# A routed expert layer on one core: five fixed experts' weights loaded from the last scores on, and TensorE's read of a tile's expert moved ahead of the wait before it

## The chip, the core and the metric

One core of one Trainium2 chip runs the kernel. The metric is the device time of one execution in microseconds; three runs of the kernel before gave 484.14, 484.23 and 485.39 us, median 484.23.

## What is computed

Two residual layers on x of 32 x 128 x 256 floats. First a gated attention over a context of the same shape, batch by batch (32 batches of 128 tokens, 16 heads of 16). Then a mixture of 14 experts over all 4096 tokens, each token going to one:

```python
x = x + tanh(g_xattn) * attention(layernorm(x), ctx, ctx)        # 16 heads, causal
h = layernorm(x).reshape(-1, 256)
logits = h @ router_w                                            # 256 x 14
weight, expert = softmax(logits) at its argmax
hid = gelu(h @ w1[expert] + b1[expert])                          # 256 -> 512
out = hid @ w2[expert] + b2[expert]                              # 512 -> 256
x = x + tanh(g_ffn) * out * weight
```

## The kernel before

The program is written engine by engine, each with its own list of instructions, and every hand-over is a semaphore. A first part runs a pipeline over the 32 batches: projections, scores, exponentials, transposed probabilities, attention, the dense layer, the router, and the token's row and name written to DRAM, sorted by expert. GpSimd scatters the names, SyncE loads inputs and stores rows.

The second part works on 39 slots (`SLOTS`). The first 25 (`FULL`) are full slots: 128 tokens of one expert. Their rows are fetched by GpSimd with an indirect DMA (`fetch`), normalised by VectorE (`norm`), transposed by TensorE (`up_in`), copied by VectorE (`up` there), multiplied by the expert's first weights (`up` of TensorE, 16 products), put through gelu by ScalarE, multiplied by the second weights (`down`, 8 products), and added up by VectorE (`start_out`, `result`), and stored by GpSimd (`store`). Slots 0 to 9 (`EARLY`) are made of the first 24 batches, so they can begin while the last batches are in attention. First weights come into a ring of R = 5 buffers (`w_ring`, 642 KB each, `load_up`); second weights of all 14 experts lie in `W2` from early on.

The last 14 slots are half slots: 64 tokens of an expert that is looked up and 64 of a fixed one, slot 25 + j taking expert j. The fixed expert's first weights, 512 KB each, are the "residents": `load_resident(e)` on SyncE puts expert e into `W1[:, e, :]`. `W1` has no memory of its own. It lies over the arena that holds the attention's buffers, expert e on columns 1024 e to 1024 e + 1023 of the arena, so a resident may be loaded only when whatever `part(n)` put on these columns is no longer used. `hold(base_ready, n)` lets SyncE wait until VectorE has begun the output of slot n - 1.

What sets the order around the change:

- SyncE's list after the last pipeline step: names of the slots 0 to 4, ring weights 0 to 4, stores 27 and 28, names of slots 5 to 9, stores 29 and 30, ring weights 5 and 6, store 31, the biases, residents 0 to 2, ring weights 7 to 9, names of slots 10 to 24, residents 3 and 4, the names of the half slots in two loads each, residents 5 to 13. It is one queue: what waits holds up all behind it.
- GpSimd's list: fetch of slot s + 5 behind the start of slot s, and the stores of results.
- TensorE's list in slots 4 to 9: `down(s)`, `up(s + 2)`, `up_in(s + 3)`. In full slots from 10 on: `up_in(s + 2)`, `up(s + 1)`, `down(s)`. In half slots: `half_up(s + 2)`, `turn(s + 1)`, `up_in(s + 3)`, `half_down(s)`.
- Every down product first reads the number of its expert from `slot_expert` or `half_expert` into a register of TensorE's sequencer (`value_load`, lines 1457 and 1506). In `down` this is ahead of its two waits, in `half_down` behind them.

Lines: 438 residents, 443 ring weights on SyncE, 424 and 432 names, 420 row stores, 595 row fetches, 604 result stores, 1078 `norm`, 1072 VectorE's `up`, 1095 `result`, 1057 the second table of slots, 1453 `up_in`, 1466 `up`, 1475 `down`, 1489 and 1491 `half_up`, 1499 `turn`, 1508 and 1511 `half_down`, 1547 the scores.

Of the kernel before, what the change touches and what calls it, by code (L numbers as in the profile page):

```python
# [7 lines left out]
P = 128  # L8
B = 32
D = 256  # L10
# [9 lines left out]
E = 14  # L20
# [114 lines left out]
def flamingo_kernel(nc, x, ctxt, gates, wq, wk, wv, wd, wd_turned, bqk, bv, bd, bd_column, rw, w1b, b1, w2, consts, out):  # L135
# [5 lines left out]
    with ExitStack() as ctx:  # L141
# [68 lines left out]
        wv_sb = part(DC * D).rearrange("p (c n) -> p c n", c=DC)  # L210
        wd_sb = part(DC * WIDE).rearrange("p (c n) -> p c n", c=DC)
# [5 lines left out]
        x_in = part(4 * D).rearrange("p (r d) -> p r d", r=4)  # L217
        c_in = part(4 * D).rearrange("p (r c s) -> p r c s", r=4, c=DC)
        x_biased = part(4 * D).rearrange("p (r d) -> p r d", r=4)
        xn = part(2 * D).rearrange("p (r d) -> p r d", r=2)  # L220
# [3 lines left out]
        k_masked = part(2 * DC * HT * P).rearrange("p (r c v s) -> p r c v s", r=2, c=DC, v=HT)  # L224
# [171 lines left out]
        def _(sp):  # L396
# [93 lines left out]
            for k in range(R):  # L490
                hold(names_loaded[k], 16)
                load_names(k, R + k)
            store(batch(29))
            store(batch(30))
            next_up(5)
            next_up(6)
# [3 lines left out]
            for e in range(3):  # L500
                load_resident(e)
# [8 lines left out]
            load_resident(3, 11)  # L510
            load_resident(4, 15)
# [4 lines left out]
            load_resident(5, 19)  # L516
            load_resident(6, 23)
            for e in range(7, E):
                load_resident(e, 26 + 3 * (e - 7) // 2)
# [911 lines left out]
        def _(pe):  # L1431
# [38 lines left out]
            def down(r, s):  # L1470
                ex = expert(s)
                pe.wait_ge(hid_t_ready, s + 1)
                wait(pe, out_ready, s - 1)
                for ch in range(FC):
                    ins = pe.matmul(y_bank[r][:, 0:D], hid_t[:, RING[r], ch, :],  # L1475
                                    W2[:, bass.ds(ex, 1), ch, :].rearrange("p e n -> p (e n)"),
                                    start=(ch == 0), stop=(ch == FC - 1))
                ins.then_inc(y_done, 1)
# [23 lines left out]
            def half_down(s):  # L1502

                pe.wait_ge(hid_t_ready, s + 1)
                pe.wait_ge(out_ready, s - 1)
                ex = pe.value_load(half_expert[0:1, s - FULL:s - FULL + 1], min_val=0, max_val=E - 1)
                for ch in range(FC):
                    pe.matmul(y_bank[s % R][0:HALF, 0:D], hid_t[:, RING[s % R], ch, 0:HALF],  # L1508
                              W2[:, bass.ds(ex, 1), ch, :].rearrange("p e n -> p (e n)"),
                              start=(ch == 0), stop=(ch == FC - 1))  # L1510
                    ins = pe.matmul(y_bank[s % R][HALF:P, 0:D], hid_t[:, RING[s % R], ch, HALF:P], W2[:, s - FULL, ch, :],
                                    start=(ch == 0), stop=(ch == FC - 1))
                ins.then_inc(y_done, 1)

            def full_slot(s):

                up_in((s + 2) % R, s + 2)
# [4 lines left out]
                down(s % R, s)  # L1522

            def mixed_slot(s):

                if s + 2 < SLOTS:
                    half_up(s + 2)
# [4 lines left out]
                if s < FULL:  # L1532
                    down(s % R, s)
                else:
                    half_down(s)
# [230 lines left out]
            down(0, 0)  # L1766
# [5 lines left out]
            down(1, 1)  # L1772
# [8 lines left out]
            down(2, 2)  # L1781
            up(4, 4)
            up_in(0, 5)
            down(3, 3)
            up(0, 5)
            lines(FULL - EARLY, 2).then_inc(slot_lines, 1)
            up_in(1, 6)

            for s in range(4, EARLY - 1):
                down(s % R, s)  # L1790
                up((s + 2) % R, s + 2)
                up_in((s + 3) % R, s + 3)
            down(4, 9)
# [57 lines left out]
```

## Time and profile before

| | us |
|---|---|
| median of three runs | 484.23 |
| the profiled execution, own time | 488.7 |
| its span, first to last instruction | 486.8 |
| TensorE matmul busy | 462.1 (95%) |
| VectorE busy | 351.3 (72%) |
| ScalarE busy | 314.2 (65%) |
| GpSimd busy | 304.5 (63%) |

The profiled execution moved 65.68 MB by DMA, 135 GB/s over its span. Its page also gives the span in 40 slices, and the slices around two thirds of the span are those in which the share of busy DMA engines rises from 0.2 to 0.8 and more, and in which TensorE's share, 0.9 or more nearly everywhere, falls to 0.8. Times in all rows are microseconds from the first instruction. PE is TensorE's matmul, PEld its weight load, PEldq its sequencer on that side, DVE VectorE, ACT ScalarE, POOL GpSimd, SPq the instructions with which SyncE issues DMAs. An entry such as `x8 [0.41 <-issue]` says eight instructions in a row, with 0.41 us of idle time before the first, ended by nothing that the profile shows.

### The profile page before, as it was taken

The page shows a single profiled execution, that of the slowest core. Times are in us where ns is not written, and L with a number is a line of the kernel's source. Part 1 is how long each engine was busy: PE and PEld are TensorE (multiplying, and loading weights), DVE is VectorE, ACT ScalarE, POOL GpSimd, SP SyncE. Part 2 cuts the span into 40 slices and gives each one's busy share as a digit, 9 for nine tenths or more (in the row PEclk, how much of TensorE's full clock was granted, in tenths as well). Part 3 has the DMA queues.
Part 4 walks back from the last instruction along what each step waited for, and adds up shares of the span by engine and source line. Part 5 has one row for each costly group of instructions (what it writes and reads, how often), then busy time and mean ns, then how long its engine had stood idle before and what let it go on. Part 6 is the DMA issues. An engine that isn't in the chain of part 4 may idle for free.

```text
span 486.8 us, 16417 instructions
## 1 busy us (share of the span) xinstructions
PE 462.1 (95%) x4775; PEld 371.3 (76%) x4775; DVE 351.3 (72%) x1128; ACT 314.2 (65%) x1481; POOL 304.5 (63%) x668
## 2 busy tenths in 40 slices
PE   8999999999999999999999998888799999999991
PEld 4888888888888888888888886776689998555540
DVE  3678999898898898998998987664345544555640
ACT  2589899889899898898898897341223322244340
POOL 5475577686776776777777676574556565445321
PEclk9899999999999999999999999998999999999997
DMA  7263566312212212212111272389778888899700
GB/s 238 78 217 134 145 179 158 54 40 47 51 37 45 52 33 52 46 32 65 34 44 36 68 213 73 92 234 290 227 222 265 259 253 247 299 300 280 243 9 7
DMA packets 38765, 65.68 MB, mean 135 GB/s; under 512 B 12457, under 2 KB 27055, under 8 KB 38704
## 3 DMA queue, kind: packets, MB, share of 16 engines
q1 hardware_dynamic: 26272, 35.33, 26.4%
q10 hardware_dynamic: 7424, 19.60, 12.6%
q0 software_dynamic: 5008, 10.01, 7.2%
q8 instruction: 29, 0.48, 0.4%
q14 instruction: 32, 0.26, 0.2%
HBM read 55.84 MB, written 9.99 MB: 135 GB/s over the span
## 4 chain that ended last, share of the span: by engine, by line
PE 80%; ACT 6%; issue 4%; DVE 4%; DMA 3%; POOL 1%; POOLq 0%; ACTq 0%; DVEq 0%
PE bank L1555 11%; PE bank L1624 10%; PE bank L1475 9%; PE bank L1466 8%; PE bank L1614 6%; ACT arena L851 5%; PE bank L1547 5%; PE bank L1508 5%; PE bank L1563 5%; PE bank L1692 5%; PE bank L1489 5%; PE bank L1610 2%; PE bank L1453 2%; PE bank L1542 2%; DMA g_rows<-token_rows,fetch_idx 2%
## 5 line engine op out<-in xcount | busy, mean ns | idle before, releaser
L851 ACT ACTIVATE arena<-bank,negmax 128x128 f32<-128x128 f32 x512 | 179.6, 403 | 13.0 <-DVE negmax L1129 13.0
L851 ACT ACTIVATION_READ_ACCUMULATOR arena<-bank,negmax 128x1 f32 x512 | 124.2, 243 | 0.0
L1129 DVE TENSOR_REDUCE negmax<-bank 128x4 f32<-128x512 f32 x128 | 84.5, 682 | 9.9 <-PE bank L1547 8.9
L1555 PE MATMUL bank<-C,arena 128*128 128x128 f32 x512 | 78.9, 277 | 1.7 <-ACT arena L851 1.2
L604 POOL DMA_INDIRECT out<-g_out,g_name x39 | 39.2, 1006 | 64.9 <-DVE g_name L1084 47.4
L809 ACT ACTIVATE hid_t<-bank,w_ring 128x128 f32<-128x128 f32 x100 | 28.5, 369 | 72.6 <-PE bank L1466 52.3
L1624 PE MATMUL bank<-arena 128*128 128x128 f32 x512 | 71.6, 283 | 0.4 <-ACT arena L877 0.2
L1555 PEld LDWEIGHTS bank<-C,arena 128*128 128x128 f32 x512 | 60.5, 141 | 12.2 <-ACT arena L851 2.4
L1624 PEld LDWEIGHTS bank<-arena 128*128 128x128 f32 x512 | 62.7, 193 | 8.0 <-issue 7.0
L1095 DVE SCALAR_TENSOR_TENSOR g_out<-bank,g_name,g_out 128x256 f32<-128x256 f32 x39 | 18.8, 483 | 59.8 <-PE bank L1475 24.6
L859 ACT ACTIVATE arena<-bank 128x512 f32<-128x512 f32 x64 | 40.8, 638 | 24.6 <-PE bank L1555 24.3
L1475 PE MATMUL bank<-W,hid_t 128*128 x200 | 49.8, 394 | 3.6 <-issue 3.5
L1466 PE MATMUL bank<-g_xt,w_ring 128*128 128x128 f32 x400 | 48.9, 275 | 1.2 <-issue 1.0
L1466 PEld LDWEIGHTS bank<-g_xt,w_ring 128*128 128x128 f32 x400 | 47.2, 192 | 2.5 <-issue 2.1
L595 POOL DMA_INDIRECT g_rows<-token_rows,fetch_idx x39 | 39.5, 1012 | 11.0 <-issue 7.1
L574 POOL DMA_INDIRECT token_names<-name,pos x32 | 34.5, 1077 | 16.6 <-issue 13.0
L1475 PEld LDWEIGHTS bank<-W,hid_t 128*128 128x128 f32 x200 | 36.9, 194 | 10.1 <-issue 5.9
L1137 DVE COPY arena<-bank 128x512 f32<-128x512 f32 x64 | 43.6, 681 | 1.4 <-PE bank L1555 0.4
L834 ACT ACTIVATE hid_t<-bank,w_ring 128x64 f32<-128x64 f32 x56 | 18.3, 327 | 37.7 <-issue 23.8
L620 POOL COPY arena<-rinv 128x128 f32<-128x128 f32 x64 | 17.1, 294 | 40.8 <-DVE rinv L1186 40.8
L583 POOL TENSOR_TENSOR arena<-arena,C 128x256 f32<-128x256 f32 x64 | 37.7, 605 | 2.5 <-ACT arena L877 2.5
L1614 PE MATMUL bank<-arena 128*128 128x270 f32 x128 | 37.1, 411 | 0.0
(179 smaller groups left out, 997.9 us busy)
## 6 DMA issues: line engine op xcount, KB each, us to landing
w_ring<-w1b ACTq DMA_DIRECT2D x15, 642.0 KB
w_ring<-w1b ACTq DMA_DIRECT2D x14, 514.0 KB
W<-w SPq DMA_DIRECT2D x14, 512.0 KB
arena<-w1b SPq DMA_DIRECT2D x14, 512.0 KB, 4.1
w_ring<-w1b SPq DMA_DIRECT2D x10, 642.0 KB
token_rows<-rows SPq DMA_DIRECT2D x32, 129.0 KB
arena<-x SPq DMA_DIRECT2D x32, 128.0 KB
arena<-ctxt SPq DMA_DIRECT2D x31, 128.0 KB, 3.8
```

Source lines behind the costliest of these rows:

```text
L583: ins = pool.tensor_tensor(k_masked[:, n.par, ch, :, :], k_t[:, ch, :].rearrange("p (o s) -> p o s", o=1).to_broadcast([P, HT, P]), const( ...
L595: pool.indirect_dma_start(out=g_rows[:, r, :], out_offset=None, in_=source, in_offset=bass.IndirectOffsetOnAxis(ap=fetch_idx[:, r:r + 1], ...
L604: pool.indirect_dma_start(out=out_rows, out_offset=bass.IndirectOffsetOnAxis(ap=g_name[:, r, 0:1], axis=0), in_=g_out[:, r, :], in_offset= ...
L851: ins = act.activation(probs[:, q, v, :], bank[q][:, v * P:(v + 1) * P], ACT.Exp, bias=negmax[:, b.par, h:h + 1], accum_out=rsum[:, b.par, ...
L859: act.activation(probs_t[:, q, :, :].rearrange("p v s -> p (v s)"), bank[4 + q % 2][:, :], ACT.Copy).then_inc(probs_t_scalar, 1)
L1129: dve.tensor_reduce(negmax[:, b.par, q * HQ:(q + 1) * HQ], bank[q][:, :].rearrange("p (v k) -> p v k", v=HQ), axis=AX_X, op=ALU.max, negat ...
L1137: dve.tensor_copy(probs_t[:, q, :, :].rearrange("p v s -> p (v s)"), bank[4 + q % 2][:, :]).then_inc(probs_t_vector, 1)
L1466: ins = pe.matmul(hid_bank[r][:, f * P:(f + 1) * P], w_ring[:, r, at:at + P], g_xt[:, RING[r], ch, :], start=(ch == 0), stop=(ch == DC - 1))
L1475: ins = pe.matmul(y_bank[r][:, 0:D], hid_t[:, RING[r], ch, :], W2[:, bass.ds(ex, 1), ch, :].rearrange("p e n -> p (e n)"), start=(ch == 0) ...
L1555: ins = pe.transpose(bank[4 + q % 2][:, v * P:(v + 1) * P], probs[:, q, v, :], ident)
L1614: ins = pe.matmul(at[:, 0:WIDE], attn_t[:, ch * P:(ch + 1) * P], wd_sb[:, ch, :], start=(ch == 0), stop=(ch == DC - 1))
L1624: ins = pe.matmul(bank[6][:, at + half_ * P:at + (half_ + 1) * P], w[:, ch, half_ * P:(half_ + 1) * P], src[:, ch, :], start=(ch == 0), st ...
```

## The change

The parts of the arena are laid out in another order, so that columns 0 to 5119, on which residents 0 to 4 go, hold only the projections' weights, the normalised x, the inputs and the masked keys. On SyncE's list, two waits (all scores done, all x tiles used) come behind the names of slots 5 to 9; residents 0 to 4 follow there, mixed with stores 29 and 30 and ring weights 5 and 6. Residents 5, 6 and 7 take the place of 3 and 4, with other slots to wait for, and 8 to 13 stand behind the half slots' names. On TensorE's list, the read of the expert in slots 3 to 9 stands ahead of `up_in`, and in slots 10 to 38 at the slot's start.

```diff
@@ -208,20 +208,20 @@
         wq_sb = part(DC * D).rearrange("p (c n) -> p c n", c=DC)
         wk_sb = part(DC * D).rearrange("p (c n) -> p c n", c=DC)
         wv_sb = part(DC * D).rearrange("p (c n) -> p c n", c=DC)
+        xn = part(2 * D).rearrange("p (r d) -> p r d", r=2)
+        x_in = part(4 * D).rearrange("p (r d) -> p r d", r=4)
+        c_in = part(4 * D).rearrange("p (r c s) -> p r c s", r=4, c=DC)
+        k_masked = part(2 * DC * HT * P).rearrange("p (r c v s) -> p r c v s", r=2, c=DC, v=HT)
         wd_sb = part(DC * WIDE).rearrange("p (c n) -> p c n", c=DC)
         rw_sb = part(DC * E).rearrange("p (c n) -> p c n", c=DC)
         bqk_sb = part(2 * DC)
         bv_sb = part(DC)
         bd_cols = part(DC)
         resid_bias = part(D)
-        x_in = part(4 * D).rearrange("p (r d) -> p r d", r=4)
-        c_in = part(4 * D).rearrange("p (r c s) -> p r c s", r=4, c=DC)
         x_biased = part(4 * D).rearrange("p (r d) -> p r d", r=4)
-        xn = part(2 * D).rearrange("p (r d) -> p r d", r=2)
         xh_t = part(4 * D).rearrange("p (r c s) -> p r c s", r=4, c=DC)
         q_t = part(2 * D).rearrange("p (r c s) -> p r c s", r=2, c=DC)
         k_t = part(D).rearrange("p (c s) -> p c s", c=DC)
-        k_masked = part(2 * DC * HT * P).rearrange("p (r c v s) -> p r c v s", r=2, c=DC, v=HT)
         values = part(4 * H * VB).rearrange("p (r e h w) -> p r e h w", r=4, e=HT, h=HG)
         probs = part(QUADS * HQ * P).rearrange("p (q v k) -> p q v k", q=QUADS, v=HQ)
         probs_t = part(QUADS * HQ * P).rearrange("p (q v s) -> p q v s", q=QUADS, v=HQ)
@@ -490,15 +490,20 @@
             for k in range(R):
                 hold(names_loaded[k], 16)
                 load_names(k, R + k)
+            hold(scores_ready, B)
+            hold(x_used, B)
+            load_resident(0)
+            load_resident(1)
             store(batch(29))
+            load_resident(2)
+            load_resident(3)
             store(batch(30))
             next_up(5)
+            load_resident(4)
             next_up(6)
             store(batch(31))
             hold(x2_ready, B)
             sp.dma_start(b1_sb[:, :], b1).then_inc(b1_loaded, 16)
-            for e in range(3):
-                load_resident(e)
             for s in range(7, EARLY):
                 next_up(s)
             for r in range(4):
@@ -507,16 +512,15 @@
             for s in range(EARLY, FULL):
                 hold(names_loaded[s % R], 16 * (s // R))
                 load_names(s % R, s)
-            load_resident(3, 11)
-            load_resident(4, 15)
+            load_resident(5, 10)
+            load_resident(6, 13)
+            load_resident(7, 16)
             hold(tables_ready, 3)
             for s in range(FULL, SLOTS):
                 hold(names_loaded[s % R], 16 * transfers(s - R, 2))
                 load_half_names(s % R, s)
-            load_resident(5, 19)
-            load_resident(6, 23)
-            for e in range(7, E):
-                load_resident(e, 26 + 3 * (e - 7) // 2)
+            for e in range(8, E):
+                load_resident(e, 19 + 5 * (e - 8) // 2)
             for k in range(SLOTS - R, SLOTS):
                 sp.wait_ge(out_stored[k % R], 16 * (k // R + 1))
 
@@ -1467,8 +1471,7 @@
                                         start=(ch == 0), stop=(ch == DC - 1))
                 ins.then_inc(hid_done, 1)
 
-            def down(r, s):
-                ex = expert(s)
+            def down(r, s, ex):
                 pe.wait_ge(hid_t_ready, s + 1)
                 wait(pe, out_ready, s - 1)
                 for ch in range(FC):
@@ -1499,11 +1502,13 @@
                     ins = pe.transpose(turned_bank[s % 2][:, ch * P:(ch + 1) * P], u_sb[:, s % 2, ch * P:(ch + 1) * P], ident)
                 ins.then_inc(hid_turned, 1)
 
-            def half_down(s):
+            def half_expert_of(s):
+                return pe.value_load(half_expert[0:1, s - FULL:s - FULL + 1], min_val=0, max_val=E - 1)
+
+            def half_down(s, ex):
 
                 pe.wait_ge(hid_t_ready, s + 1)
                 pe.wait_ge(out_ready, s - 1)
-                ex = pe.value_load(half_expert[0:1, s - FULL:s - FULL + 1], min_val=0, max_val=E - 1)
                 for ch in range(FC):
                     pe.matmul(y_bank[s % R][0:HALF, 0:D], hid_t[:, RING[s % R], ch, 0:HALF],
                               W2[:, bass.ds(ex, 1), ch, :].rearrange("p e n -> p (e n)"),
@@ -1514,15 +1519,17 @@
 
             def full_slot(s):
 
+                ex = expert(s)
                 up_in((s + 2) % R, s + 2)
                 up((s + 1) % R, s + 1)
                 if s == FULL - 2:
                     half_up(FULL)
                     up_in((s + 3) % R, s + 3)
-                down(s % R, s)
+                down(s % R, s, ex)
 
             def mixed_slot(s):
 
+                ex = expert(s) if s < FULL else half_expert_of(s)
                 if s + 2 < SLOTS:
                     half_up(s + 2)
                 if s + 1 < SLOTS:
@@ -1530,9 +1537,9 @@
                 if s + 3 < SLOTS:
                     up_in((s + 3) % R, s + 3)
                 if s < FULL:
-                    down(s % R, s)
+                    down(s % R, s, ex)
                 else:
-                    half_down(s)
+                    half_down(s, ex)
 
             def scores(b):
 
@@ -1763,13 +1770,13 @@
             pe.wait_ge(logits_summed, 31)
             attend(last)
             pe.wait_ge(experts_loaded, 16 * E)
-            down(0, 0)
+            down(0, 0, expert(0))
             pe.wait_ge(attn_ready, B)
             dense(last, bank[7])
 
             up(2, 2)
             up_in(3, 3)
-            down(1, 1)
+            down(1, 1, expert(1))
             up(3, 3)
             up_in(4, 4)
 
@@ -1778,19 +1785,22 @@
             pe.wait_ge(seen_ready, 30)
             ranks().then_inc(mixed_done, 1)
             counts(bank[7][:, 0:E], pair=True).then_inc(counts_done, 1)
-            down(2, 2)
+            down(2, 2, expert(2))
             up(4, 4)
+            ex = expert(3)
             up_in(0, 5)
-            down(3, 3)
+            down(3, 3, ex)
             up(0, 5)
             lines(FULL - EARLY, 2).then_inc(slot_lines, 1)
+            ex = expert(4)
             up_in(1, 6)
 
             for s in range(4, EARLY - 1):
-                down(s % R, s)
+                down(s % R, s, ex)
                 up((s + 2) % R, s + 2)
+                ex = expert(s + 1)
                 up_in((s + 3) % R, s + 3)
-            down(4, 9)
+            down(4, 9, ex)
             for s in range(EARLY, FULL - 1):
                 full_slot(s)
                 if s == EARLY + 4:
```

## Rows read from the trace of the kernel before

**Rows 1.** Stretch, length, busy PE PEld DVE ACT POOL (xcount), granted clock, DMA share, GB/s:

```profile
320.00:325.00 5.00, 4.28 (x28) 3.63 (x28) 4.42 (x27) 3.31 (x7) 3.20 (x7) 1.00 1.07 217
325.00:330.00 5.00, 2.98 (x25) 2.45 (x23) 2.02 (x9) 0.00 (x0) 3.81 (x6) 1.00 0.97 334
330.00:335.00 5.00, 3.96 (x11) 2.76 (x12) 1.44 (x5) 1.14 (x4) 3.02 (x4) 0.66 1.00 294
...
360.00:370.00 10.00, 10.00 (x74) 9.39 (x73) 5.68 (x21) 2.92 (x11) 5.61 (x8) 1.00 0.80 248
```

**Rows 2.** TensorE in order of time: start, duration, idle before in brackets:

```profile
323.58 1.99 PE L1475 MATMUL bank<-W,hid_t 128*128 x8 [0.43 <-issue]
...
329.07 0.44 PE L1453 MATMUL bank<-C,g_xn 128*128 128x128 f32 x2 [1.54 <-DVE g_xn L1078]
330.01 3.55 PE L1475 MATMUL bank<-W,hid_t 128*128 x8 [0.50 <-issue]
334.59 2.02 PE L1466 MATMUL bank<-g_xt,w_ring 128*128 128x128 f32 x16 [1.03 <-issue]
...
347.98 0.44 PE L1453 MATMUL bank<-C,g_xn 128*128 128x128 f32 x2 [2.31 <-issue]
...
353.32 1.99 PE L1475 MATMUL bank<-W,hid_t 128*128 x8 [0.41 <-issue]
...
357.80 1.99 PE L1475 MATMUL bank<-W,hid_t 128*128 x8 [0.42 <-issue]
...
361.63 1.89 PE L1475 MATMUL bank<-W,hid_t 128*128 x8
...
365.37 1.89 PE L1475 MATMUL bank<-W,hid_t 128*128 x8
```

**Rows 3.** The chain that ended last: start, duration, what; slot 6:

```profile
319.11 8.55 DMA g_rows<-token_rows,fetch_idx
```

**Rows 4.** Reads of the expert: ns minimum/median/maximum, first to last start:

```profile
L1457 PEldq TENSOR_LOAD <-slot_table x25: 296/308/478, 307.1 to 415.6; - x25
L1457 PEldq FUSED_REGOPS  x25: 151/151/165, 307.6 to 416.0; - x25
...
L1506 PEldq TENSOR_LOAD <-half_table x14: 297/301/313, 420.3 to 474.2; - x14
```

**Rows 5.** SyncE's DMA issues in order of time, first start and length:

```profile
290.64 4.75 SPq L424 DMA_DIRECT2D slot_names<-token_names  x5
296.27 10.89 SPq L420 DMA_DIRECT2D token_rows<-rows  x2
310.47 6.70 SPq L443 DMA_DIRECT2D w_ring<-w1b  x2
...
318.16 1.43 SPq L438 DMA_DIRECT2D arena<-w1b  x3
320.64 11.11 SPq L443 DMA_DIRECT2D w_ring<-w1b  x3
```

**Rows 6.** VectorE's waits between 325 and 336 us: total, times, longest:

```profile
DVE slot_table L1057 <- remote: 2.1, 1, 2.1
DVE g_xt L1072 <- remote: 1.6, 1, 1.6
```

**Rows 7.** All engines in order of time: last scores, fetch and norm of slot 2:

```profile
294.24 1.09 PE L1547 MATMUL bank<-arena 32*128 32x256 f32 x16
...
297.46 1.09 POOL L595 DMA_INDIRECT g_rows<-token_rows,fetch_idx  x1 [0.29 <-POOL fetch_idx L593]
...
305.62 0.41 DVE L1078 TENSOR_SCALAR g_xn<-g_rows 128x256 f32<-128x256 f32 x1
```

**Rows 8.** In order of time: weight loads at a tile change; last half slot:

```profile
285.47 0.23 PEld L1542 LDWEIGHTS bank<-later_bf,rows_of_bf 32*128 32x128 bf16 x16 [0.17 <-issue]
...
430.44 0.13 PEld L1508 LDWEIGHTS bank<-W,hid_t 128*64 128x64 f32 x1 [0.17 <-issue]
...
474.99 0.42 PE L1508 MATMUL bank<-W,hid_t 128*64 x1 [0.48 <-issue]
```

## The prediction, made before the kernel was run

> **What bounds the kernel now.** I first read the busy time by stretches of 5 to 10 us, then TensorE's instructions in order of time with the idle time in front of each, then the chain of work that ended last, and last the load queue of SyncE. Outside one stretch TensorE has no room: from 360 us on it is busy in every stretch, a full slot takes 3.74 us from one down product to the next (365.37 - 361.63) and no idle time stands in front of its down product [rows 1, 2]. The room is between 325 and 358 us, slots 3 to 9. There TensorE is busy 2.98 of 5 us and the granted clock falls to 0.66 in the next stretch, while the DMA engines are busy 0.97 to 1.00 of the time [rows 1]. The reader is to see three kinds of loss. The first is one fetch of token rows that took 8.55 us and ends in 1.54 us of idle TensorE [rows 2, 3]; behind it come a down product of 3.55 us at the half clock, where the same product takes 1.99 us in slots 8 and 9, and 1.03 us before the next up product [rows 2]. The second is 2.31 us in front of the transpose of slot 9 [rows 2]. The third is small and repeats: each of the six down products of slots 4 to 9 has 0.41 to 0.50 us of idle time "issue" in front of it (the first and the last two of the six are shown) [rows 2]. That is the read of the expert's number: a load of 308 ns and register work of 151 ns on TensorE's sequencer [rows 4], which in those slots stands between two transposes of 0.44 us and the down product, so nothing queued covers it.
>
> **The change, part by part.** Durations are of the profiled execution, 488.7 us with a span of 486.8; I take the sum of gains off as it is and apply it to the median of 484.23, which is 4.5 us under the profiled time. No term is scaled.
>
> *Three residents leave the crowd.* Before, SyncE sends three residents from 318.16, right behind the ring weights of slot 6, the last store and the biases, and ahead of the ring weights of slots 7 to 9 [rows 5]. The fetch of slot 6 is issued at 319.11 [rows 3]. By the shapes in the code, what stood in front of it is 642 + 129 + 28 + 3 x 512 KB = 2335 KB; the change leaves 799 KB. If the time goes with what is in front, 8.55 x 799 / 2335 = 2.9 us, and the rows are there at 322.0, long before VectorE comes to them: VectorE's normalisation at 328.60 had waited for them, and it feeds the transpose at 329.07 [rows 2]. So the 1.54 us go. The two hand-overs that VectorE saw late, 2.1 us before the table of slots and 1.6 us before the copy of slot 6, lie in the same full stretch [rows 6]; with the 1.54 us of idle gone I expect no fall of the clock either, which gives 3.55 - 1.99 = 1.56 us, and the up product at 334.59 no longer waits its 1.03 us [rows 2]. Together 1.54 + 1.56 + 1.03 = 4.13 us. The bounds are 0 (the crowd is made by ring weights and fetches alone) and 4.13; I take 4.13, because the wait ends with a DMA in the chain itself [rows 3].
>
> *The 2.31 us before slot 9.* No instruction in the profile explains why VectorE began its result so late there, and at that time no resident was under way: the three had been issued by 319.6 and slots 7 to 9 by 331.8 [rows 5]. The bounds are 0 and 2.31; I take 0 gained, since the moved loads are not near, and keep 2.31 for the range.
>
> *The residents' new place.* Five residents, 2560 KB, are now sent from the moment that SyncE has sent the names of slots 5 to 9 (290.64 + 4.75 = 295.39) and the last scores are done: the last of the score products starts at 294.24 and lasts 1.09 us, to 295.33 [rows 5, 7]. The two ends meet, so the new wait holds nothing up on SyncE; behind it in the queue stand only stores 29 and 30, the first of which went at 296.27 [rows 5]. Two residents go ahead of store 29, two behind it, one behind the weights of slot 5 (310.47) [rows 5]. What can suffer is the fetch of slot 2, issued at 297.46 and read by VectorE at 305.62, because TensorE's transpose of slot 2 is in front of the attention product of the last batch [rows 7]. In front of it will be 4 x 512 + 129 = 2177 KB. From the row of 8.55 us that is 8.55 x 2177 / 2335 = 8.0 us, landing at 305.4, just in time; at the slowest rate of any full stretch, 217 GB/s [rows 1], 2177 x 1024 bytes would take 10.3 us, landing at 307.7, 2.1 us late. Below, nothing can be gained here, since the old fetch was in time. I take 0, from the nearer row, and keep 2.1 us. Of the stores nobody reads before all 32 have landed. The fifth resident lies between the weights of slots 5 and 6, each needed a slot or more later.
>
> *Residents 5 to 13* go out by base_ready 10, 13, 16, and later, instead of 19 and up. They sit in the same places of SyncE's queue relative to the names, and the half names behind resident 7 still wait for the third table. In the full slots this is one resident more than before; at 248 GB/s and no idle TensorE [rows 1] that stage has cover, and in the half slots it is three transfers fewer, where TensorE also waits for nothing. I cost both at nothing. If the cover were gone, a late fetch would cost as much as the 1.54 us row [rows 2].
>
> *The expert read ahead.* In slots 4 to 9 the read now stands before the transposes, in time in which the sequencer waits for VectorE's normalisation, and behind 16 up products that are already queued. All six gaps go: 0.50 + 4 x 0.41 or 0.43 + 0.42; I count 6 x 0.43 = 2.58 us. In slot 3 the 0.43 us before 323.58 [rows 2] go too, but the work behind it waits for VectorE's tables, so it counts 0. Bounds: 0 and 3.01. In full slots the read was hidden behind the up products and stays hidden, 0 [rows 2]. In the half slots, the 0.17 us before each down product [rows 8] are no read: the same 0.17 us stand before products of another tile shape with no register read near them [rows 8]. So 0 for twelve of the fourteen. The last one is different: the read begins at 474.2, when the last activation releases it [rows 4], and TensorE has 0.48 us idle before 474.99 [rows 8]. This lies on the end of everything, and the read is now done before: 0.48 us.
>
> The Trainium skill's page "DMA: Bandwidth & Descriptors", section "Latency and other measured facts", gives a floor of about 600 ns for such a load; the rows show 308 and 151 ns [rows 4], and by the page the six would be 3.6 us.
>
> *The sum:* 4.13 + 0 + 0 + 2.58 + 0.48 = 7.19 us. 484.23 - 7.19 = 477.0 us. What is late next: in slots 4 to 9 the transpose waits for VectorE's normalisation, so the period should go from 4.48 us (357.80 - 353.32) to about 4.07, not to 3.74.
>
> **The rivals.** (A) The forecast, 477.0. (B) The 2.31 us go as well, because everything in that stage is at other times and less is in flight: 474.7. For it: the late hand-overs stand only in this stage. (C) The fetches were late not by what stood in front of them but by the total traffic, which the change does not lower; then only the reads count, 2.58 + 0.48 = 3.06, giving 481.2. For it: ring weights alone keep the engines at 0.8 of their time later on [rows 1]; against it: those stretches have no idle TensorE. (D) The residents' part comes as forecast, but the reads in slots 4 to 9 give nothing, since the transposes before them wait for VectorE and VectorE's chain becomes the bound: 4.13 + 0.48 = 4.61, giving 479.6. Against it: VectorE's chain starts at the end of the down product and so moves with it. (E) Slower: the burst of 2 MB catches the fetch of slot 2 with twice the latency of the one row, 17.1 us. It lands at 314.6, 9.0 us after 305.62, TensorE idles and adds the 1.56 us of half clock, 10.6 in all; against the gain of 7.2 that is 3.4 us slower, 487.6. It decides from a latency of 13.8 us (8.16 + 7.19 - 1.56); against it stands 8.55 us behind a larger heap. (F) At about that latency, or with a resident late in the full slots, the two cancel, 484.
>
> The Trainium skill's page "DMA: Bandwidth & Descriptors", section "Queues, rings and completion order", says that a DMA engine goes round the queues that have work, one packet of each in turn. By that rule GpSimd's fetch would pass the heap on SyncE's queue, the moved residents would neither have delayed it nor delay the fetch of slot 2, and the result would be near rival C. The trace's 8.55 us for one fetch speaks against it, so C is not given more than below.
>
> **How the numbers follow.** Chances: A 0.45, B 0.20, C 0.13, D 0.10, E 0.06, F 0.06. The likeliest gives 477.0. The range reaches from under B (474.7, less a period that gets nearer to 3.74) to over C (481.2), so 473.5 to 481.5; E and F are left out. Differences under 0.3% (1.5 us) can hardly be told from no change in this kernel. A to D are faster by more than that: 0.88; F is the same, 0.06; E is slower, 0.06.
>
> **What would show it.** Right: no stretch between 318 and 350 us with less than 4 of 5 us of TensorE; no half clock there; down products of slots 4 to 9 some 4.07 us apart with no "issue" gap of 0.4 us; the first product of the first all-full stage (361.63 before) near 355; the last half slot without its 0.48 us. Wrong: idle TensorE before the transpose of slot 2 near 305 us; a fetch that still takes 8 us at slot 6; the half clock after it; a new wait for weights or rows in the full slots, or for a resident at the first products of a half slot.

## The result and the profile after

Twelve executions of the changed kernel gave a median of 482.94 us (481.58 to 484.29), twelve of the kernel before beside them 485.06 (483.71 to 486.75). The ratio is 0.9953, with a 95% interval of 0.9937 to 0.9969: about 2.3 us faster. (This ratio and those below are not the quotients of the two medians beside them: here that is 0.9956, for the reads alone below 0.9900 where the ratio is 0.9916.) The profiled execution took 482.4 us with a span of 480.6. The forecast was 477.0 us, the end of its range 481.5.

The same stretches as in [rows 1], of the changed kernel; length, busy PE, PEld, DVE, ACT, POOL, granted clock, DMA share, GB/s:

```profile
320.00:325.00 5.00, 4.77 (x34) 4.28 (x33) 4.50 (x25) 2.43 (x5) 3.75 (x6) 1.00 0.82 93
325.00:330.00 5.00, 4.17 (x31) 3.69 (x30) 1.43 (x5) 1.14 (x4) 3.84 (x7) 1.00 1.10 309
330.00:335.00 5.00, 0.62 (x3) 0.62 (x4) 1.93 (x6) 0.59 (x3) 1.86 (x2) 0.73 0.77 210
335.00:340.00 5.00, 5.00 (x21) 4.28 (x20) 1.73 (x5) 0.55 (x3) 3.03 (x5) 0.59 0.92 274
340.00:345.00 5.00, 5.00 (x36) 4.59 (x35) 2.18 (x7) 1.69 (x7) 3.80 (x5) 1.00 0.60 165
```

The hole of [rows 1] is not filled. It has come together: TensorE stands still from 329.2 to 334.4 us, the granted clock is 0.73 and 0.59 in the 5 us stretches of the 330s, and from 340 us on there is no room at all. TensorE in order of time, changed kernel, answering [rows 2] (L1457 is `up_in`, L1470 `up`, L1478 `down`; the down products are those of slots 3 to 10):

```profile
321.40 1.93 PE L1478 MATMUL bank<-W,hid_t 128*128 x8
...
325.50 1.89 PE L1478 MATMUL bank<-W,hid_t 128*128 x8
327.23 1.95 PE L1470 MATMUL bank<-g_xt,w_ring 128*128 128x128 f32 x16
334.38 0.69 PE L1457 MATMUL bank<-C,g_xn 128*128 128x128 f32 x2 [5.21 <-DVE g_xn L1082]
334.87 3.62 PE L1478 MATMUL bank<-W,hid_t 128*128 x8
338.28 2.35 PE L1470 MATMUL bank<-g_xt,w_ring 128*128 128x128 f32 x16
...
340.68 1.89 PE L1478 MATMUL bank<-W,hid_t 128*128 x8
...
344.62 1.93 PE L1478 MATMUL bank<-W,hid_t 128*128 x8
...
348.46 1.92 PE L1478 MATMUL bank<-W,hid_t 128*128 x8
...
352.29 1.92 PE L1478 MATMUL bank<-W,hid_t 128*128 x8
...
356.05 1.89 PE L1478 MATMUL bank<-W,hid_t 128*128 x8
```

Part of what was forecast is there. The transpose of slot 6, which had waited 1.54 us for its rows, stands without idle time ahead of the down product at 325.50. No "issue" gap is left in slots 3 to 9. The down products of slots 6 to 10 are 3.76 to 3.94 us apart, against the 4.48 of [rows 2]. The last half slot, which starts at 468.76, has lost its 0.48 us. But the next transpose, that of slot 7, waits 5.21 us, and the down product and up products behind it run at the half clock: 3.62 - 1.92 = 1.70 and 2.35 - 1.95 = 0.40 us more than usual. Who holds it up is seen on VectorE: first its list in order of time (nothing stands between the two lines), then the chain that ended last in that stretch.

```profile
326.14 0.40 DVE L1076 COPY g_xt<-bank 128x256 f32<-128x256 f32 x1
332.19 0.17 DVE L1088 COPY g_name<-slot_names 128x2 int32<-128x2 int32 x1 [5.65 <-DMA out<-g_out,g_name]
```

```profile
324.14 8.03 DMA out<-g_out,g_name
```

L1088 is `start_out(5)`. It writes slot 5's output into buffer 5 % R = 0 and so waits until the result of slot 0 has been stored. GpSimd issues that store at 324.14, behind the last names, and it takes 8.03 us. Behind `start_out(5)` on VectorE's list are the result of slot 4 and the normalisation that TensorE's transpose wants. The five residents went at 294.03, 295.36 and 309.49 (these are SyncE's issues, [rows 5] before):

```profile
294.03 0.81 SPq L438 DMA_DIRECT2D arena<-w1b  x2
...
295.36 1.21 SPq L438 DMA_DIRECT2D arena<-w1b  x2
...
309.49 0.43 SPq L438 DMA_DIRECT2D arena<-w1b  x1
```

Between the two profiled executions lie 6.2 us of span. From the down product of slot 2 to that of slot 10 it is 42.98 us before (318.65 to 361.63 [rows 2]) and 38.93 after (317.12 to 356.05), 4.05 less. From there to the last half slot it is 0.65 less (113.36, 112.71). The other 1.5 us stand ahead of slot 2 and are no effect of the change: the first down product starts at 308.05 before and at 306.68 after, and at 306.45 in a kernel below that has nothing changed up to there; it is at 308.21 in another (ten buffers, e4) that is the changed kernel up to there. The median moved by 2.1 us only, because the profiled execution of before, 488.7 us, is longer than every one of the 63 executions of that kernel that were timed beside this and the kernels below (482.65 to 487.61).

### The profile page after: what moved, and what is told of

Read it like the earlier page. It is cut to its first block, busy times and chain, and to the rows that moved or that the text cites. A ratio compares the mean times of both kernels' runs of the same rounds, so it can differ in the third digit from the quotient of the medians.

```text
span 480.6 us, 16418 instructions
## 1 busy us (share of the span) xinstructions
PE 458.5 (95%) x4775; PEld 370.5 (77%) x4775; DVE 351.6 (73%) x1128; ACT 314.1 (65%) x1481; POOL 305.0 (63%) x668
## 4 chain that ended last, share of the span: by engine, by line
PE 79%; ACT 5%; DVE 5%; issue 4%; DMA 3%; POOL 2%; SPq 1%; POOLq 0%; DVEq 0%; ACTq 0%
PE bank L1562 11%; PE bank L1631 10%; PE bank L1478 8%; PE bank L1470 7%; PE bank L1621 6%; ACT arena L855 5%; PE bank L1554 5%; PE bank L1513 5%; PE bank L1570 5%; PE bank L1492 5%; PE bank L1699 5%; PE bank L1617 2%; PE bank L1549 2%; PE bank L1457 2%; PE bank L1502 2%
## 5 line engine op out<-in xcount | busy, mean ns | idle before, releaser
L1478 PE MATMUL bank<-W,hid_t 128*128 x200 | 49.4, 392 | 0.5 <-issue 0.3
L1470 PE MATMUL bank<-g_xt,w_ring 128*128 128x128 f32 x400 | 49.2, 276 | 0.2 <-DVE g_xt L1076 0.2
L1470 PEld LDWEIGHTS bank<-g_xt,w_ring 128*128 128x128 f32 x400 | 47.9, 193 | 1.0 <-issue 0.4
L1478 PEld LDWEIGHTS bank<-W,hid_t 128*128 128x128 f32 x200 | 37.2, 196 | 5.3 <-issue 1.0
```

Of the source, the lines that this page charges most:

```text
L1470: ins = pe.matmul(hid_bank[r][:, f * P:(f + 1) * P], w_ring[:, r, at:at + P], g_xt[:, RING[r], ch, :], start=(ch == 0), stop=(ch == DC - 1))
```

## The experiments

**One half of the change each.** The reads alone, with arena and SyncE's list as before:

```diff
             for s in range(4, EARLY - 1):
-                down(s % R, s)
+                down(s % R, s, ex)
                 up((s + 2) % R, s + 2)
+                ex = expert(s + 1)
                 up_in((s + 3) % R, s + 3)
...
             def full_slot(s):
 
+                ex = expert(s)
                 up_in((s + 2) % R, s + 2)
...
```

> The kernel before with only TensorE's part of the change: the reads of the expert ahead, arena and residents as before. Theory (the read-ahead works by itself, and its gaps lay on the path): 7 gaps of 0.4 us and 0.5 us at the last half slot, so 2.5 to 3 us faster than before (ratio about 0.994). Rival (slots 3 to 9 are paced by the stores and fetches, and TensorE only waits somewhere else): the 0.5 us of the last half slot alone, ratio 0.999; the gaps vanish in the profile and come back in front of the transposes.

Measured: 480.04 us, ratio 0.9916 (0.9890 to 0.9942). The residents alone, the reverse: new arena and SyncE's list, and on TensorE `ex = expert(s)` back in `down`:

> The changed kernel with TensorE's reads put back where they were: arena and residents alone. Theory (the residents' move ends the late fetch of slot 6, but the store of slot 0 that VectorE waits for at slot 5 becomes late instead): 0 to 1 us faster than before, an idle time of several us before the transpose of slot 7, ended by the normalisation behind that store. Rival (the residents' part brings most of the 2.1 us and the reads nothing): 2 us faster.

Measured: 484.82 us, ratio 1.0005 (0.9986 to 1.0024). So the gain is the reads', some 4.1 us, and the residents alone bring nothing, to within 0.9 us. With the residents moved as well as the reads 0.37% seems lost again (0.9953 against 0.9916), though the two intervals overlap. TensorE in order of time, reads alone (6's transpose, down of slot 4, up of slot 6, 7's transpose, down of slot 5):

```profile
326.89 0.44 PE L1453 MATMUL bank<-C,g_xn 128*128 128x128 f32 x2 [1.83 <-DVE g_xn L1078]
327.17 2.77 PE L1474 MATMUL bank<-W,hid_t 128*128 x8
329.73 2.80 PE L1466 MATMUL bank<-g_xt,w_ring 128*128 128x128 f32 x16
333.83 0.44 PE L1453 MATMUL bank<-C,g_xn 128*128 128x128 f32 x2 [1.31 <-DVE g_xn L1078]
334.11 1.92 PE L1474 MATMUL bank<-W,hid_t 128*128 x8
```

and residents alone:

```profile
326.02 1.89 PE L1479 MATMUL bank<-W,hid_t 128*128 x8
...
333.46 0.44 PE L1457 MATMUL bank<-C,g_xn 128*128 128x128 f32 x2 [3.77 <-DVE g_xn L1082]
334.31 3.13 PE L1479 MATMUL bank<-W,hid_t 128*128 x8 [0.41 <-issue]
```

The transpose of slot 7 comes at 333.83, 333.46 and, in the changed kernel, at 334.38. All three are set by one date, the landing of slot 0's store (331.5, 331.2, 332.2 us). With the residents where they were, slot 6's late rows used up 1.83 us of the time until then; with them moved TensorE comes to slot 7 earlier and waits longer. The two waits were in a row in front of one date, so taking the first away brought nothing.

**The order of the stores.** The changed kernel, with the store of slot 0 ahead of a fetch and the last names on GpSimd:

```diff
             refetch(6)
+            store(0, 0)
             refetch(7)
             names(batch(31))
-            store(0, 0)
```

> The changed kernel with one line moved on GpSimd: the store of slot 0's result is sent behind the fetch of slot 6, ahead of the fetch of slot 7 and the last names, about 4 us earlier. Theory (VectorE's wait for that store is what ate the gain: 5.65 us of idle time, ended by a DMA that took 8.0 us from 324.14): the wait shrinks by about 4 us and the half clock behind it may go, so 3 to 5.5 us faster than the changed kernel, 478 to 480 us. Rival (the stage is paced by the whole DMA traffic, whatever waits first): under 1 us, 482 to 483.

Measured: 480.86 us, 0.9934 (0.9913 to 0.9955). The chain now goes through the next store, that of slot 1:

```profile
324.62 6.33 DMA out<-g_out,g_name
```

Its buffer is wanted by `start_out(6)`, and TensorE still idles 3.27 us in front of slot 7's transpose, with a down product of 3.35 us behind it. One store earlier mostly uncovers the next: 3 to 5.5 us had been expected, and the ratio is 0.2% under that of the changed kernel, with overlapping intervals.

**Ten buffers for results.** The changed kernel with `O = 2 * R` buffers of `g_out`, `g_name` and `out_stored`:

```diff
+O = 2 * R
-        g_out = sb("g_out", [P, R, D])
+        g_out = sb("g_out", [P, O, D])
...
-                wait(dve, out_stored[r], s // R * 16)
+                wait(dve, out_stored[s % O], s // O * 16)
...
```

> The changed kernel with ten output buffers and names instead of five, so that the output of slot s waits for the store of slot s - 10 and not s - 5; GpSimd's order is not changed. Theory (the wait for the store of slot 0): it is gone altogether, and with it up to 5.2 us of idle TensorE and 1.6 us at the half clock: 476 to 479 us. Rival (whole traffic): the fetches or the ring weights become the wait at the same place, 482 to 483.

Measured: 478.81 us, 0.9886 (0.9858 to 0.9915). TensorE around slot 8's transpose, the longest idle time between 320 and 345 us:

```profile
335.54 0.44 PE L1458 MATMUL bank<-C,g_xn 128*128 128x128 f32 x2 [0.99 <-DVE g_xn L1083]
335.81 1.92 PE L1479 MATMUL bank<-W,hid_t 128*128 x8
```

The 5.21 us and the half clock are gone, and 3 us of time with them (0.9953, 0.9886): the wait for the buffer is the cause of both. The store is as slow as it was (6.85 us from 325.67); only nobody waits for it.

**The clock alone.** The changed kernel with 20 products of 128 x 512 that nobody reads, put in front of slot 7's transpose (`keep_warm` is a helper that the kernel has already; it gets the bank as an argument here):

```diff
                 ex = expert(s + 1)
+                if s == 4:
+                    keep_warm(20, bank[2])
                 up_in((s + 3) % R, s + 3)
```

> The changed kernel with 20 products that nobody reads (128 x 512, 16 bit) in front of TensorE's transpose of slot 7, where it idles 5.2 us. Theory (the changed kernel loses to the reads-only one mainly by the half clock, 6.8 us of it after the one long idle time against 3.4 us): no half clock there, 2 us faster than the changed kernel, 480.5 to 481.5. Rival (the clock costs little, since at that place the engine waits for rows and stores anyway): 482.5 to 484.

Measured: 481.38 us, 0.9911 (0.9884 to 0.9937).

```profile
330.52 4.48 PE L1726 MATMUL bank<-ones_bf 128*128 128x512 bf16 x20
335.70 0.44 PE L1457 MATMUL bank<-C,g_xn 128*128 128x128 f32 x2 [0.70 <-DVE g_xn L1082]
335.98 1.92 PE L1478 MATMUL bank<-W,hid_t 128*128 x8
```

The wait for the store is as long as before, but the clock stays at its upper level (2.4 GHz) and the down product takes 1.92 us instead of 3.62. From the down product of slot 4 to that of slot 6 it is 339.81 - 327.00 = 12.81 us, against 340.68 - 325.50 = 15.18. With this the changed kernel is where the reads alone were (0.9916). The traces say the same: from slot 7's transpose to slot 10's down product it is 21.67 us in the changed kernel (334.38 to 356.05), 19.51 in the reads alone (333.83 to 353.34) and 19.43 here (335.70 to 355.13). So what the residents cost beside the reads is, in the main, the clock. In the reads alone it falls too, but in the products in front of the wait for the store (2.77 us at 327.17, 2.80 at 329.73), where there was time to lose; in the changed kernel it falls behind that wait, where there is none.

**What makes the DMAs slow.** The changed kernel, with the scatters of the names of batches 28 to 31 bounded so that they write nothing. It leaves out these four batches' tokens in the routed experts' later slots:

```diff
...
-                scatter_name(g.back(1))
-                scatter_name(g)
+                limit = dict(bounds_check=0, oob_is_err=False) if g.n > 28 else {}
+                scatter_name(g.back(1), **limit)
+                scatter_name(g, **limit)
```

> The changed kernel with the last four scatters of names (batches 28 to 31) bound to position 0, so that GpSimd issues them as before but they write nothing; the tokens of these batches are left out of the result, and slots 0 to 9 are not touched by that. Theory (the small writes of the names slow all other transfers for 3 to 4 us each time, and the residents do not): the store of slot 0, 8.0 us in the changed kernel, takes 3 to 5 us, TensorE's 5.2 us of idle time before the transpose of slot 7 fall under 2, no long stretch at the half clock, 477 to 479 us. Rival (what fills the DMA engines there is ring weights, fetches and row stores): 7 us or more for that store, 482 to 483 us.

Measured: 478.44 us, 0.9857 (0.9824 to 0.9889). The gain stands where it was expected: from slot 2's to slot 10's down product 33.34 us (318.45 to 351.79) for the changed kernel's 38.93, and from there to the end 124.5 us in both, so the tokens left out gain nothing later on. The same edit in the kernel before, with the same part left out:

> The kernel before, with the name scatters of batches 28 to 31 bounded so that they write nothing (it leaves out the tokens of these four batches in the routed experts' later slots). Theory N (the late DMAs of 319 to 335 us come from the name writes): the fetch of slot 6 takes under 5 us instead of 8.55, no idle TensorE over 0.7 us before up_in of slot 6, no half clock in slots 3 to 9, and the time is 1.4 to 3.5 us under before, 0.993 to 0.997. Theory T (the forecast's: the heap of loads in front, three residents among it, makes them late): the fetch still takes over 7 us, and the time stays within 0.3% of before.

Measured: 483.23 us, 0.9978 (0.9961 to 0.9994). Three stretches of 2 us in the changed kernel, columns as above:

```profile
322.00:324.00 2.00, 2.00 (x15) 1.84 (x14) 1.73 (x9) 1.40 (x5) 1.53 (x2) 1.00 0.92 73
...
328.00:330.00 2.00, 1.17 (x11) 0.98 (x9) 0.00 (x0) 0.00 (x0) 1.42 (x4) 1.00 1.17 170
330.00:332.00 2.00, 0.00 (x0) 0.00 (x0) 0.00 (x0) 0.00 (x0) 1.70 (x2) 1.00 0.71 103
```

and with the names unwritten (e5):

```profile
322.00:324.00 2.00, 1.79 (x10) 1.47 (x10) 1.79 (x10) 1.69 (x3) 1.23 (x3) 1.00 0.86 276
...
328.00:330.00 2.00, 2.00 (x18) 1.92 (x17) 1.54 (x5) 0.33 (x2) 1.42 (x3) 1.00 0.76 235
330.00:332.00 2.00, 1.93 (x13) 1.61 (x12) 0.92 (x3) 1.14 (x4) 1.73 (x3) 1.00 1.01 263
```

With the names unwritten the engines move 3.8 and 1.4 times as much in the first two of these stretches, at a lower busy share, and 2.6 times as much in the third, at 1.01 for 0.71. The two executions are not in step: the first down product starts at 306.68 in the changed kernel and at 307.97 in e5. The kernel with the clock kept up (e7) writes its names and starts at 308.19, in step with e5:

```profile
322.00:324.00 2.00, 1.78 (x11) 1.48 (x10) 1.79 (x10) 1.50 (x2) 1.36 (x4) 1.00 1.15 103
324.00:326.00 2.00, 2.00 (x16) 1.90 (x15) 1.79 (x11) 0.93 (x4) 1.39 (x3) 1.00 0.72 100
```

e5 moved 276 and 400 GB/s in these two. The difference is in the packets of the others. These are SyncE's loads (queue q1) between 322 and 324 us, packets, MB and share of the 16 engines, first in e7 and then in e5:

```profile
q1 hardware_dynamic: 19, 0.10, 75.3%
```

```profile
q1 hardware_dynamic: 97, 0.50, 77.3%
```

At the same share of the engines there are a fifth of the packets, 1.27 us each instead of 0.26 us (0.753 or 0.773 of 16 x 2 us, divided by their number). In the kernel before the effect is smaller: in 320 to 322 and 322 to 324 us it moved 265 and 185 GB/s, and 315 and 342 with the names unwritten (e8). In all thirteen profiles the time from issue to landing goes like this (us):

| | fetch of slot 6 | store of slot 0 |
|---|---|---|
| residents at the old place (before, e1, e6, e9, e11) | 7.92 to 9.22 | 6.60 to 8.05 |
| residents moved (after, e2, e3, e4, e7, e10) | 5.46 to 6.21 | 6.85 to 8.03 |
| old place, names unwritten (e8) | 6.64 | 5.66 |
| moved, names unwritten (e5) | 4.53 | 2.70 |

(e6, e9, e10 and e11 follow below.) By single pairs the heap in front of the fetch was worth 2.3 us of its time (8.55 before, 6.21 after) or 2.1 (6.64, 4.53), the name scatters 1.9 or 1.7. For the store, which is what VectorE waits for, the moved heap is worth nothing while the names are written and 3.0 us when they are not (5.66, 2.70), and the names are worth 0.9 to 2.4 us at the old place and 4.2 to 5.3 at the new. (In the trace of before many landings are missing: its 8.55 rests on 6 of 16 records, its 6.78 on one.) The expectation for e8 had put the fetch at under 5 us by the names alone; 6.64 says that both work. It had also said that no idle time over 0.7 us would stand before slot 6's transpose: none does, but slot 7's waits 2.52 us for the store and the clock falls to 0.82 in 330 to 335 us and 0.50 in 335 to 340 us. The time had been expected at 0.993 to 0.997; 0.9978 is between that and no change.

**Buffers without residents.** The reads alone with ten output buffers:

> The kernel before with the reads ahead and ten output buffers; arena and residents as before. Theory (the residents' new place brings nothing and the old one costs nothing, because VectorE waits for the store of slot 0 and not for the residents' crowd): as fast as the changed kernel with ten outputs, 478 to 480 us. Rival (once the wait for the store is gone the fetch of slot 6, late behind the old residents, is the next bound and the new place does pay): 1.5 to 3 us slower than that, 480 to 482 us.

Measured: 480.04 us beside 485.65, 0.9897 (0.9867 to 0.9927). This stands beside other runs of before than e4 did (0.9886) and doesn't decide between the two expectations, so the next three stand beside the same ones. Ten output buffers and nothing else:

> The kernel before with ten buffers for results and their names instead of five, and nothing else. If buffer reuse is late only once another wait has gone (what the changed kernel showed), before gains nothing by it: 0.998 to 1.002. If it was already part of the loss in before (VectorE's late hand-overs), 0.993 to 0.996.

Measured: 481.85 us, 0.9955 (0.9934 to 0.9977). Ten buffers on the changed kernel again:

> The changed kernel with ten output buffers, side by side with the next one, which has the old places of the residents and the reads ahead. If the residents' new place gives something once the buffers are free: 0.984 to 0.988, and at least 0.3% under the next. If it gives nothing: both the same within 0.2%, near 0.989.

Measured: 478.95 us, 0.9902 (0.9876 to 0.9928). And on the reads alone again:

> The kernel before with the reads ahead and ten output buffers, old arena and old places of the residents. Residents worth something: 0.990 to 0.992, above the run beside it. Residents worth nothing: near 0.989, the same as the run beside it.

Measured: 478.54 us, 0.9890 (0.9861 to 0.9918). The buffer was already part of the loss before the change: ten of them bring 0.45% on their own, as much as the whole change does. TensorE with ten buffers and nothing else:

```profile
326.01 0.44 PE L1454 MATMUL bank<-C,g_xn 128*128 128x128 f32 x2 [0.20 <-DVE g_xn L1079]
326.87 1.99 PE L1476 MATMUL bank<-W,hid_t 128*128 x8 [0.42 <-issue]
...
331.39 1.99 PE L1476 MATMUL bank<-W,hid_t 128*128 x8 [0.41 <-issue]
```

Slot 6's rows took 7.92 us here with the residents at the old place, and the transpose waits 0.20 us for them, not 1.54. Each of the "issue" gaps is still there, and no half clock. With the buffers free the reads are worth 481.85 - 478.54 = 3.3 us by the medians. The profiled executions show much less of it (36.23 us from slot 2 to slot 10 in e9, 35.55 in e11), for in e11 slot 6's transpose waits 2.16 us for its rows and a down product of 3.19 us follows; but that execution, 481.03 us, is the longest of its six. The residents' new place is worth nothing that can be measured in the whole time even then (0.9902 against 0.9890), though the stretch is shorter with it (34.44, 35.55). The chains of both go on through the last names. The chain of the changed kernel with ten buffers (e10):

```profile
322.64 7.67 DMA token_names<-name,pos
...
331.24 6.46 DMA slot_names<-token_names
```

and of the reads alone with ten buffers (e11):

```profile
323.84 8.64 DMA token_names<-name,pos
...
333.42 6.21 DMA slot_names<-token_names
```

The best kernels here are these with reads ahead and ten buffers, near 0.989, whichever place the residents have.

## Why the prediction was wrong

*The direction and the reads: right.* Moving the reads took all the "issue" gaps, and the period went below the 4.07 us forecast, to 3.76 to 3.94. Reads alone brought 0.84%, 4.1 us, against 3.06 with the last half slot; the interval (0.26% to either side, 2.8 to 5.3 us) holds the forecast, and beside free buffers they brought 3.3. From slot 10 to the last half slot it was 0.65 us for 0.48. Rival D (reads worth nothing) is refuted by e1. The reads in the sequencer's row are the same 0.30 us each as in [rows 4]; they are hidden, not shorter.

*The residents' 4.13 us: the step that failed.* Measured alone they brought nothing (1.0005, 0.9986 to 1.0024). The prediction read [rows 3] rightly as far as the wait went: the fetch got shorter and the 1.54 us went. It failed in what it said next. "What is late next" was answered with the normalisation's own period; the answer was the store of slot 0. In the trace of before it is issued at 325.73 and lands at 332.5 (the one landing of it that the trace has):

```profile
325.73 1.00 POOL L604 DMA_INDIRECT out<-g_out,g_name  x1 [0.30 <-issue]
```

No wait for it shows there, since the late hand-over in front of `start_out(5)` (L1084) ends only at 334.02 [rows 6]:

```profile
334.02 0.42 DVE L1072 COPY g_xt<-bank 128x256 f32<-128x256 f32 x1 [1.62 <-remote]
334.36 0.16 DVE L1084 COPY g_name<-slot_names 128x2 int32<-128x2 int32 x1
```

But `start_out(5)` needs buffer 0 free, and whoever had listed the landing of each DMA of the stage against its reader would have found two dates in a row, 327.7 for the rows and 332.5 for the store. What comes ahead of `start_out(5)` can gain no more than the time by which that step came behind its own date: 334.36 - 332.5 = 1.9 us there, not 4.13, and nothing in the reads alone, where VectorE waits 3.2 us for the store although slot 6's rows are still late.

Two parts of the 4.13 us had no shown cause in the first place. The 1.03 us before the up product and VectorE's two late hand-overs "remote" were put down to the crowd because they lay in the same stretch. In none of the other twelve profiles, four of them with the crowd and the names as before, is there idle time before an up product between 318 and 346 us or such a hand-over.

*The clock.* 1.56 us were booked as a gain because the idle time would go. It had not gone, it had grown to 5.21 us, and the half clock cost 1.70 + 0.40 us at a place without cover. e7 prices it: 0.9953 to 0.9911, with intervals that just meet.

*The latency of a fetch by the bytes in front of it.* 8.55 x 799 / 2335 = 2.9 us was forecast; 5.5 to 6.2 was measured. The bytes in front are only one part: 2.1 to 2.3 us by the pairs above, beside 1.7 to 1.9 for the names, and 4.53 us are left without either. In front of slot 2's fetch the same scaling gave 8.0 us; it took 6.3, against 2.8 to 2.9 in the kernels with the residents at the old place (e1, e6, e8, e9, e11). The rule of the Trainium skill's page "DMA: Bandwidth & Descriptors", section "Queues, rings and completion order", that an engine serves its queues in turn packet by packet, would have let GpSimd's DMAs pass the heap on SyncE's queue, as the prediction worked out. The traces agree only in part: the fetches of slots 6 and 2 are 1.7 us and more later with the heap than without, and so is the store when the names are unwritten (5.66, 2.70). Only the store with the names written takes as long either way (6.60 to 8.05, 6.85 to 8.03).

*Rival C* named 481.2 us and "only the reads count". It was the nearest, but not for its reason: the fetch did get shorter, and what stood in the way was the store. It also missed that with the residents moved the reads bring less.

*The hand-over before slot 9.* None of the other twelve profiles has idle time there. The prediction kept it as no gain, which did no harm to the sum, but it was a sign that the profiled execution was an unusual one: e2, whose median equals that of before, needs 40.09 us from slot 2 to slot 10 where the profile of before needs 42.98. The prediction read 4.13 us from an execution 3.6 us above the median of the runs beside the changed kernel (488.7, 485.06) and took them off a median, with no term scaled.

*A miscount.* By the two lists of SyncE the full slots get two residents more than before (six for four) and the half slots four fewer, not one and three. Both were costed at nothing, and the time from slot 10's down product to the last half slot has only become shorter (112.71 for 113.36), so nothing hung on it.

*The residents' new place: right in its result.* The fetch of slot 2 was issued at 296.09 and had landed at 302.36, its rows were normalised at 304.26, and the transpose has the 0.35 us of idle time it also had without the burst. Rival E is refuted.

```profile
304.26 0.41 DVE L1082 TENSOR_SCALAR g_xn<-g_rows 128x256 f32<-128x256 f32 x1
...
304.72 0.44 PE L1457 MATMUL bank<-C,g_xn 128*128 128x128 f32 x2 [0.35 <-DVE g_xn L1082]
```

*Open:* that reads and residents together are worse than the reads alone rests on 0.9953 against 0.9916, two intervals that overlap, on e7 and on the lengths in the traces. By how much exactly wasn't settled. Why the profiled execution of before was so long is open too. Nor was it tried to write the names in another way, with all of them kept.

## What to carry to other kernels

Before a wait is booked as a gain, list what the same engine waits for next and when that lands: taking the first of two waits away gains no more than the time by which the step behind the second comes later than its date, and the reuse of an output buffer is such a date as much as a load is. Work of a sequencer that stands between a wait and the product it is for (0.4 us per slot here) costs nothing when it is moved ahead of the wait; here this paid with the residents at either place (1.0005 to 0.9953, and 0.9916 alone) and with ten buffers. A fall of the clock in front of a date that is waited for anyway is covered, one behind it is paid in full; compare the kernel with a version in which the idle time is filled. And hold the profiled execution against the median before its idle times are added up.

## What the runs showed of the hardware

Small scattered writes slowed the other DMAs in flight. Four scatters of 128 names of 8 bytes are next to nothing in bytes, but with them written the core moved 103 and 100 GB/s in two stretches of 2 us, at a busy share of 1.15 and 0.72 (e7), and without them 276 and 400 GB/s at 0.86 and 1.00 (e5); a packet of SyncE's loads took 1.27 us and 0.26; a store of 128 rows took 6.85 to 8.03 us and 2.70. With the residents at their old place it was less: 265 and 185 GB/s against 315 and 342. The Trainium skill's page "DMA: Bandwidth & Descriptors", section "Specifications", says that below 512 bytes an engine reads, modifies and writes; that the transfers of other queues are slower beside such writes is what the traces add; that it is by this reading and writing was not tested. Which part of the way is shared (engine or memory) no run here shows.
